# A decoder layer with experts: tokens sorted by kind for the middle layer, the row copies moved to ScalarE, and a memset between the result gathers

## The reference

```python
x = x + attn(_layernorm(x), wq, wk, wv, wo ...)      # 16 heads of 128, weights = codes * block scales
x = x + xattn(_layernorm(x), token_ids, ctx, ctx, ctx)
x = x + ffn(_layernorm(x), router_w, bias, w_gate, w_up, w_down, sw_gate, sw_up, sw_down)

# xattn: a feed-forward with 4 experts; the token's id picks one (the same ctx[e] serves as Wg, Wu, Wd)
expert_ids = min(clip(token_ids, 0, 12499) // 3125, 3)
for e in range(4):
    y = (silu(h @ ctx[e].T) * (h @ ctx[e].T)) @ ctx[e].T     # 256 -> 256 -> 256
    out = where(expert_ids == e, y, out)

# ffn: 32 experts 256 -> 128 -> 256, the best 4 of each token by sigmoid(h @ router_w.T) + bias,
# weighted by their scores over the scores' sum, plus one shared expert for all tokens
```

## Time and profile before

| | |
|---|---|
| median of 3 runs | 532.93 us (532.72 to 533.77) |
| the profiled execution | 531.99 us, its span 530.3 us |
| busy, share of the span | PE 94%, DVE 80%, ACT 55%, POOL 38% |
| bytes moved by DMA | 57.01 MB |

### The profile page before, as it was taken

How to read it: one execution, slowest core, us unless ns; L and a number is a source line. 1 busy time by engine, 2 the same in 40 slices (tenths; PEclk the granted TensorE clock), 3 DMA queues, 4 the chain that set the end, 5 groups by cost and what they waited for, 6 DMA issues and landing times.

```text
span 530.3 us, 11470 instructions
## 1 busy us (share of the span) xinstructions
PE 499.6 (94%) x3274; PEld 443.8 (84%) x3274; DVE 422.2 (80%) x1046; ACT 289.3 (55%) x793; POOL 201.5 (38%) x233
## 2 busy tenths in 40 slices
PE   7799999999999999999999998899987799999997
PEld 6688899899899899898898897678975588888886
DVE  6589988988988988988988987874688586677555
ACT  2566656656656655656666556254444244455552
POOL 3318621611612513513503600064510466627662
PEclk9999999999999999999999999999999999999999
DMA  6361311210210211211200792199921155436665
GB/s 192 99 170 40 92 32 32 69 30 30 69 30 30 69 30 30 69 30 30 69 0 1 257 323 96 26 296 305 297 69 41 43 147 159 160 110 184 192 187 166
DMA packets 59411, 57.01 MB, mean 108 GB/s; under 512 B 4128, under 2 KB 57072, under 8 KB 59248
## 3 DMA queue, kind: packets, MB, share of 16 engines
q1 hardware_dynamic: 55936, 48.03, 30.2%
q0 software_dynamic: 3168, 8.42, 6.1%
q10 hardware_dynamic: 272, 0.13, 0.1%
HBM read 46.21 MB, written 18.74 MB: 122 GB/s over the span
## 4 chain that ended last, share of the span: by engine, by line
PE 67%; DVE 19%; ACT 6%; issue 5%; POOL 1%; DVEq 0%; ACTq 0%; POOLq 0%
PE bank L791 14%; PE bank L792 13%; PE bank L793 13%; PE bank L965 11%; PE bank L973 5%; DVE rmax L1394 3%; DVE qk_lo L1386 3%; DVE nmax L1398 3%; PE bank L871 3%; ACT qk_hi L1190 2%; ACT prob L1198 2%; DVE pT_lo L1426 2%; PE bank L1146 1%; PE bank L969 1%; PE bank L797 1%
## 5 line engine op out<-in xcount | busy, mean ns | idle before, releaser
L1198 ACT ACTIVATE prob<-bank,nmax 128x256 f32<-128x256 f32 x128 | 59.5, 470 | 107.7 <-DVE nmax L1398 107.7
L607 POOL TENSOR_TENSOR w_lo<-st_c,w_hi 128x512 fp32r<-128x512 f32 x32 | 41.3, 1289 | 194.3 <-ACT w_hi L1161 194.3
L965 PE MATMUL bank<-moe_w,xT 128*128 x252 | 65.2, 381 | 1.2 <-DVE xT L1622 1.2
L1386 DVE SCALAR_TENSOR_TENSOR qk_lo<-bank,b_col,qk_hi 128x512 fp32r<-128x512 f32 x64 | 47.9, 748 | 16.0 <-ACT qk_hi L1190 15.3
L791 PE MATMUL bank<-hT_hi,w_lo 128*128 128x512 f32 x128 | 52.8, 413 | 5.8 <-DVE qk_lo L1386 2.9
L1394 DVE TENSOR_REDUCE rmax<-bank 128x2 f32<-128x512 f32 x64 | 43.9, 686 | 14.2 <-PE bank L793 14.1
L965 PEld LDWEIGHTS bank<-moe_w,xT 128*128 128x128 f32 x252 | 45.4, 190 | 6.8 <-issue 1.6
L689 POOL DMA_INDIRECT x_in<-h_dram,source x32 | 32.4, 1011 | 48.4 <-DVE source L1574 28.1
L792 PE MATMUL bank<-hT_lo,w_hi 128*128 128x512 f32 x128 | 50.7, 396 | 0.0
L793 PE MATMUL bank<-hT_hi,w_hi 128*128 128x512 f32 x128 | 50.4, 394 | 0.0
L1190 ACT ACTIVATE qk_hi<-bank,b_col 128x512 fp32r<-128x512 f32 x64 | 44.0, 687 | 7.7 <-PE bank L793 6.2
(11 more groups left out here) (219 smaller groups left out, 1543.3 us busy)
## 6 DMA issues: line engine op xcount, KB each, us to landing
y_dram<-ysb SPq DMA_DIRECT2D x63, 128.0 KB, 2.5
moe_w<-in_w_gate SPq DMA_DIRECT2D x8, 512.0 KB, 8.4
moe_w<-in_w_up SPq DMA_DIRECT2D x8, 512.0 KB, 7.6
moe_w<-in_w_down SPq DMA_DIRECT2D x4, 1024.0 KB, 8.8
st_c<-in_wq_codes SPq DMA_DIRECT2D x16, 128.0 KB
st_c<-in_wk_codes SPq DMA_DIRECT2D x16, 128.0 KB
st_c<-in_wv_codes SPq DMA_DIRECT2D x8, 256.0 KB
st_c<-in_wo_codes SPq DMA_DIRECT2D x8, 256.0 KB
```

The lines of the kernel that those rows point to most:

```text
L965: mm = pe.matmul(o, xT_of(kt), w, start=kt == 0, stop=kt == KT - 1)
L1198: ex = act.activation(prob[:, i % 4, qt, :], bS[i % 2][:, qt * S:(qt + 1) * S], ACT.Exp, bias=nmax[:, i % 2, qt:qt + 1], scale=SCALE, accu ...
L1386: dve.scalar_tensor_tensor(out=qk_lo[:, hp, m, n * HALF:(n + 1) * HALF], in0=src[:, :], scalar=b_col[:, bass.ds(g_h + m * H, 1)], in1=qk_h ...
```

## The change

**Sorting.** The token ids are loaded one for each partition and tile. GpSimd compares them (`kinds`), TensorE ranks them by matmuls with ones in the last attention group (`token_ranks`), GpSimd works out for each token its place in its half sorted by kind (`places`) and the borders of the kinds (`segments`). When a pair of residual tiles is complete, GpSimd scatters its rows with indirect DMAs to `xs_dram` in sorted order (`scatter`), and SP reads the tiles back into `x_acc`. VectorE then normalizes the first half after attention instead of between its last tiles; TensorE runs some matmuls whose result nobody uses meanwhile (`keep_warm`).

**The middle layer** has 14 segments (`NSEG`), 7 for each half: at each border of two kinds a tile is computed once for each. ScalarE copies the segment's tile (`segment_copy`, by a register), TensorE does 6 matmuls of 256 columns with the kind's weights, ScalarE silu, VectorE one operation with the segment's mask, TensorE two transposes (`mid`), ScalarE and VectorE split, TensorE 6 matmuls of 256 columns, VectorE adds to the residual (`routed_sum`). GpSimd only writes its constants. Normalization statistics are spread over the segments; half of the normalization for the third layer runs on GpSimd (`ln_pool`), and some square roots become powers on GpSimd (`ln_root`).

**The router** builds `in_slot` in four parts; the last shared-expert steps are placed behind the first row transpose and around the first expert product.

**The expert steps.** The row copies go to ScalarE. The store count lags one store instead of two (`AFTER`). Since the tokens are sorted now, the residual and the tables are written to `x2_dram` in trip 2 and gathered back by 8 indirect DMAs in the token's order, after which `order`, `slots_ordered`, `last_slots` and `tiles_needed` run, in trip 4 (`TABLE_TRIP`) instead of 1 and 2.

**The result gathers** wait for other product counts, and between two of them GpSimd clears one column and waits for that.

The diff, cut to its core:

```diff
+        BESIDE = 38
+            def own(ins):
+                done[0] += 1
+                ins.then_inc(p_own, 1)
+                pool.wait_ge(p_own, done[0])
...
+            def scatter(half):
+                pool.wait_ge(p_dest, 1)
+                for t in range(half * HT, (half + 1) * HT):
+                    if t % 2 == 0:
+                        pool.wait_ge(v_w, Plan(G - 1).w_done_count(t // 2, True))
+                    pool.indirect_dma_start(out=xs_dram, out_offset=bass.IndirectOffsetOnAxis(ap=dest[:, t:t + 1], axis=0),
+                                            in_=x_acc[:, t, :], in_offset=None).then_inc(d_xs[half], 16)
...
             for n in range(ROWS):
-                wait(pool, t_x, n - AHEAD + 1)
+                wait(pool, t_x, n - min(STEPS, 4 + n // 6) + 1)
                 pool.indirect_dma_start(out=xg[:, n % STEPS, :], ...
+            pool.wait_ge(d_x2, 16)
+            for t in range(NT):
+                pool.wait_ge(t_gu, SH + 3 * STEPS + t * 7 // 8)
+                pool.indirect_dma_start(out=x_all[:, t, :], out_offset=None, in_=x2_dram, ...
             pool.wait_ge(v_slot, S_NEED)
             for n, (t, k) in enumerate(gather_order):
+                if n > 0:
+                    own(pool.memset(quiet[:, :], 0.0))
                 if k == 2:
                     pool.wait_ge(t_x, ROWS)
                 if k == 3:
                     pool.wait_ge(v_sh, NT)
-                wait(pool, t_gu, SH + BESIDE + n)
+                pool.wait_ge(t_gu, SH + min(USED, BESIDE + n * 7 // 8))
                 if t % 2 == 0:
                     apart(pool)
                     pool.reg_load(at[0:2], need[0:1, k * NT + t:k * NT + t + 2])
...
# SP
+            for half in range(NH):
+                sp.wait_ge(d_xs[half], 16 * HT)
+                for t in range(half * HT, (half + 1) * HT):
+                    sp.dma_start(x_acc[:, t, :], xs_dram.rearrange("(t p) d -> t p d", p=P)[t]).then_inc(d_xa[t], 16)
             sp.wait_ge(v_w, 4 * G + 1)
+            sp.wait_ge(p_seg, 1)
...
# TensorE, middle layer
             def pre(n):
+                pe.wait_ge(a_copy, n + 1)
+                wait(pe, v_t, n - 1)
                 for kt in range(KT):
+                    mm = mm3(Z_AT[n % 2][:, 0:D], h_seg[:, n % 2, kt * P:kt * P + P], h_seg[:, n % 2, (KT + kt) * P:(KT + kt) * P + P],
+                             kind_part(cT_hi, n, kt), kind_part(cT_lo, n, kt), kt == 0, kt == KT - 1)
+            for n in range(NSEG + 2):
+                if n < NSEG:
+                    pre(n)
+                if n == NSEG:
+                    ln_tensor(pe, 2, 0, ENDS[0])
+                if 1 <= n <= NSEG:
+                    mid(n - 1)
+                if n >= 2:
+                    post(n - 2)
+                if n == SEGS - 2:
+                    ln_tensor(pe, 1, 1, ENDS[1])
...
# VectorE, middle layer
+            for n in range(NSEG):
+                routed_product(n)
+                if n >= 1:
+                    routed_low(n - 1)
+                if n >= 2:
+                    routed_sum(n - 2)
+                beside(n)
...
# VectorE, trips
+            trip(TABLE_TRIP, 0, False, {2: (table_back, lambda: order(0), lambda: order(2)),
+                                        3: (lambda: order(4), lambda: order(6), slots_ordered),
+                                        5: (last_slots,), 7: (tiles_needed,)})
...
# ScalarE, trips
+            def row_copy(j):
+                wait(act, t_x, j + 1)
+                act.copy(xT_all[:, :, j * SLOTS:(j + 1) * SLOTS],
+                         bX[j % 2][:, 0:D].rearrange("p (k s) -> p k s", k=KT)).then_inc(a_row, 1)
```

More of the change, by code:

```diff
@@ L50 @@
 ROW_TRIPS = ROWS // STEPS
-LAST_TRIP = 2
+TABLE_TRIP = 4
 HOT = NT // 2
@@ L572, in store @@
                         stored(u - AFTER + STEPS, it - 1)
-            store(0)
-            with sp.Fori(1, TRIPS - 1) as it:
+            for it in range(ROW_TRIPS):
+                store(it)
+            with sp.Fori(ROW_TRIPS, TRIPS - 1) as it:
                 store(it)
@@ L911, in _, with load_kinds @@
             over_groups(pe, body)
-            def zero(half):
-                for yb in ENDS[half]:
-                    pe.matmul(yb[:, :], zeros[:, :], zeros[:, 0:1].to_broadcast([1, HALF]), start=True, stop=True)
+            at = [pe.alloc_register(f"at{i}") for i in range(STEPS)]
+            def load_kinds(w):
+                apart(pe)
+                pe.reg_load(at[w % 2 * PACK:w % 2 * PACK + PACK],
+                            seg_expert[0:1, :, :].rearrange("p h i -> p (h i)")[:, w * PACK:(w + 1) * PACK])
@@ L1322, in _, with trip @@
                     shared_silu(n + 3)
+                if n >= SH - 3 and n < SH - 1:
+                    row_copy(n - SH + 3)
                 shared_copy(n)
-            def trip(it, first, last):
+            def trip(it, first, last, rows=0):
                 steps = LAST if last else STEPS
@@ L1328, in trip @@
                     j = it * STEPS + u
+                    if u < rows and j > 0:
+                        row_copy(j + 1)
                     if u < steps:
@@ L1406, in body @@
             def body(pl):
-                for i in range(PAIRS + (DRAIN + 2 if pl.last else 0)):
+                for i in range(PAIRS + (DRAIN + 1 if pl.last else 0)):
                     if i < PAIRS and not (pl.first and i == 0):
@@ L1446, in body @@
-                    if pl.last and i == PAIRS + 3:
-                        ln_low(dve, 1, 0, ENDS[0])
-            over_groups(dve, body)
-            statistics, variances, reciprocals, rows = ln_vector(dve, 1, 1, x_acc)
-            dve.wait_ge(v_w, 4 * G + 1)
+                    if pl.last and i == 2:
+                        dve.wait_ge(t_rank, 1)
+                        dve.tensor_copy(ranked[:, :], bO[0][:, S:S + NROUTE * NT + NROUTE * NH]).then_inc(v_rank, 1)
+                    if pl.last and i == 4:
+                        dve.wait_ge(p_bounds, 1)
+                        for half in range(NH):
+                            ins = dve.max(sorted_b[:, half, :], bounds[:, half, :])
+                        ins.then_inc(v_sorted, 1)
@@ new lines, in routed_low, with routed_sum @@
+            def routed_low(n):
+                dve.wait_ge(a_g, n + 1)
+                wait(dve, t_y, n - 1)
+                dve.tensor_tensor(gu_lo[:, n % 2, :], TURN_AT[n % 2][:, 0:D], gu_hi[:, n % 2, :], ALU.subtract).then_inc(v_g, 1)
+            def routed_sum(n):
+                row = dve.snap(at[word(n) % STEPS], min_val=0, max_val=(NT - 1) * (D + 2 * TOPK))
+                dve.wait_ge(t_y, n + 1)
+                wait(dve, v_y, n)
+                here = x_all[:, :, :].rearrange("p t d -> p (t d)")[:, bass.ds(row, D)]
+                apart(dve)
+                dve.tensor_tensor(here, y_at(n), here, ALU.add).then_inc(v_y, 1)
@@ L1452, in _ @@
+            norm = {(n, half): ln_vector(dve, n, half, x_acc) for n, half in LN_KINDS[2:]}
+            statistics, variances, reciprocals, rows = norm[1, 0]
             statistics()
             variances()
+            for tile in Plan(G - 1).of_slot(PAIRS + DRAIN, 1):
+                proj_low(Plan(G - 1), *tile)
             reciprocals()
@@ L1480, in _ @@
[L1480 to L1485 removed]
+                if n >= 2:
+                    routed_sum(n - 2)
+                beside(n)
+            routed_low(NSEG - 1)
+            routed_sum(NSEG - 2)
+            sums_ready(1, HT - 2)
+            routed_sum(NSEG - 1)
+            sums_ready(1, HT - 1)
@@ L1486, in _ @@
+            for part in norm[2, 1][1:]:
                 part()
@@ L1688, in add_shared, with trip @@
                 dve.tensor_tensor(x_acc[:, t, :], shared[:, t, :], x_acc[:, t, :], ALU.add).then_inc(v_sh, 1)
-            def trip(it, rows, last, beside, between={}):
+            def trip(it, rows, last, beside):
                 steps = LAST if last else STEPS
```

589 lines of the change are left out of this document (397 added, 192 removed).

## The result

The changed kernel takes **548.75 us** (median of four runs, 548.14 to 549.16) beside 533.35 us for the kernel before: a ratio of **1.0275, 95% interval 1.0232 to 1.0319**, slower. The profiled execution has a span of 546.9 us against 530.3.

What follows compares the result with a forecast made beforehand. TensorE, busy 94% of the span, was taken as the bound. Terms 4.0 - 19.9 - 4.8 = -20.7 us, plus 34.7 for the result gathers, on 531.99 profiled gave 546.0; median forecast 546.9 us, range 513 to 553.

Steps and rivals of the forecast that it cites:

- Part 1: End of attention: scatter, read-back, normalization and transposes ahead of the first middle matmul cost +4.0 us, bounds +1 and +6.
- Part 2: Middle layer: 14 segments take 30 us instead of 49.9, a gain of 19.9; bounds 26.5 and 36 us.
- Part 3: Router: spread statistics, slot masks in four parts and moved shared-expert steps gain 4.8 us of 31.3; bounds -2.5 and -6.
- Part 4: Expert steps: row copies, reordering gathers, table store and VectorE's table work all lie beside TensorE, so no change.
- Part 5: Result gathers on GpSimd: waiting for the memset exposes each gather's lead, pitch 2.3 us instead of 1.25, TensorE +34.7 us.
- TensorE's wait, 34.4 us: Last products: TensorE asks for the last gather at 526.4, it lands at 560.8; 0.3 us more for the restart.
- Rival 1: Result gathers: the lead stays hidden, pitch 1.25 to 1.55 us, time 514 to 523 us; chance 0.23.
- Rival 2: Middle layer: segments of 2.6 us make it 39 us, 556 in all; chance 0.07 together with Rival 3, over 553.
- Rival 3: Scatter and read-back waits drop TensorE's clock to 1.2 GHz for half the middle: 559 us; chance 0.07 together with Rival 2.

Runs made afterwards that it cites:

- the sequencer's own wait: Changed kernel with the memset left out but semaphore and wait kept, GpSimd's sequencer adding to the semaphore itself: 0.9977 of the kernel before (0.9954 to 1.0001).

## Why the prediction was right, and where not

The forecast was 546.9 us and the range 513 to 553, with slower at 0.68. The time is 548.75, 1.9 us above the forecast and 4.2 inside the range, and the mechanism is the one named. By its own steps:

- **Part 1, +4.0 us.** Measured +3.7: first middle matmul at 345.11, 345.4 forecast. The landings, booked at 2.9 us each, took 2.4 and 2.2 in the median, and the first transpose came at 340.80 instead of 341.6; from there to the first matmul it took 4.3 us instead of 3.8.
- **Part 2, 30 us.** Measured, to the start of the last add as in the 49.9 before, 375.29 - 345.11 = 30.2. Undisturbed segments, from 360 us on, are 1.64 us apart, where I had 1.75 to 1.8, and the early ones beside VectorE's normalization 1.95 to 2.85, where I had 2.1.
- **Part 3, 26.5 us.** Measured 402.15 - 375.29 = 26.9. The power on GpSimd, which I booked at nothing (+-0.3), takes 1.03 us, and from `var` to the use of its result it is 377.81 - 376.49 = 1.32. The root and reciprocal of the kernel before take 394.99 - 394.34 = 0.65 for the same:
```profile
394.34 0.17 DVE L728 TENSOR_SCALAR var<-mv 128x4 f32<-128x4 f32 x1
...
394.99 0.16 DVE L736 TENSOR_TENSOR nt<-rstd 128x4 f32<-128x4 f32 x1
```
  So that term was mis-sized by 0.7 us. This is read from rows; no run swapped the two. The net shift at the first expert product is 20.4 us, against 20.7.
- **Part 4, nothing.** This step failed, by 1.5 us. From the first to the last expert product it is 95.7 us against 94.2 before. VectorE's table work, which I booked as lying beside TensorE, comes in pieces of 1 us between the copies that the next product waits for; steps beside it are 1.9 us apart instead of 1.63 (418.71, 420.62, 422.50). That it fits beside TensorE is true of the mean and not of each step: the pieces are as long as VectorE's free time in a step, or longer. This is read from the timeline alone; the four slowest steps (416.79 to 424.58) make up 1.3 of the 1.5 us.
- **Part 5, pitch 2.3 us, bounds 1.9 and 2.5.** Measured 2.262, with an odd lead of 0.85 (I took 1.1) and an even one of 1.46 (1.44). The mean came nearer than its parts, because some even tiles take up to 1.9. The first gather was forecast at 486.5 - 20.7 = 465.8 and came at 468.40, 2.6 us late: the steps ahead lost up to 1.5 us, the shift ahead of them was 20.4 and not 20.7, and it starts 1.9 us after the table and not 1.4. The last was forecast at 537.1 and came at 538.53; TensorE starts on it at 541.38, 2.85 later, 3.0 forecast.
- **TensorE's wait, 34.4 us, and what stands behind it.** The waits for gathers sum to 30.6 us, but their sum is the wrong thing to compare: TensorE does part of its products between them, some at the lower clock, and neither moves the end. What sets the end is the last gather and the work behind it. Forecast: it lands at 560.8 - 20.7 = 540.1, and 4.2 us follow (530.3 - 526.4, and 0.3 for the restart), so 544.3. Measured: 541.38 and 5.5 us, 546.9. The products behind the last gather take 544.31 - 541.38 = 2.93 us; in the kernel without the memset, at a clock of 1.0, they take 512.91 - 511.36 = 1.55. So **1.4 us** is the lower clock, a term that I had put at nothing. (In the changed kernel's second trace, on the other chip, it is 544.21 - 541.90 = 2.31, so 0.8 us: there the eight products before still ran at 1.00.) My error: I had thought of the clock as a rival of the middle layer only, and not of the 30 us wait that my own forecast contained.

The span is 2.6 us above the forecast, 1.3 ahead of the last landing and 1.3 behind it. The 1.3 ahead are a first gather that comes 2.6 us late, less 31 x (2.3 - 2.262) = 1.2 for the pitch and 0.15 for the landing. The median misses by only 1.9, because I had added 0.9 for its distance from the profiled execution and it was 0.2. So part of the closeness is luck: in the pitch a lead 0.25 us too long for odd tiles met even tiles that sometimes take longer, and the clock's 1.4 us met smaller misses the other way.

Rival 1, at 514 to 523, needed the lead to stay hidden behind the wait for the own memset. The kernel without memset gives 518.0 us, so its price was right; its condition, a lead that stays hidden, doesn't hold. The rule that spoke for it, in the Trainium skill, "Perfetto Trace Analysis", on the SWDGE DMA instruction, says that the sequencer hands an instruction over and goes on to the next. The back-to-back gathers and the sequencer's own wait (0.30 us of gap) agree with it; the 0.85 us behind every late wait shows that the rule can't be stretched over a wait that isn't fulfilled yet. Rival 2 had no part: the middle took 30.2 us. Rival 3 didn't happen where it was looked for, because the change fills those waits with matmuls; with them taken out the clock fell there, and the middle took about 1 us longer.

## What to carry to other kernels

A wait cost nothing here where it was already fulfilled (gap 0.30 us), and little between small operations (0.08 us); ahead of an indirect DMA, and ending at the last moment, it cost 0.85 us and more. So before putting a wait between two DMAs of one engine, look for rows in which that engine was released by a semaphore, and count the gap after the release once per wait, not the length of the small operation. A constant gap whose releaser changes from row to row is such a lead. And when the sum of a forecast has a long wait on TensorE in it, the work behind the last such wait belongs in the sum at the lower clock (1.4 us here); slow work between waits only takes from the next wait.

## What the runs showed of the hardware that I had not expected

- Behind a wait that ends late, GpSimd's indirect DMA starts 0.85 us after the work waited for has ended, in every kernel that has the pair, for memsets of 0.11 and 0.33 us alike, and 1.46 with a register load in between. Behind a wait already fulfilled it starts 0.30 us after the gather ahead, and a memset of 0.12 us fits into that gap for nothing.
- After 25.5 us without work, eight products took 3.65 us instead of 1.99; 4 us later the clock was back, and four took 1.03. Waits of 2.30 and 1.95 us with eight products between brought it down again: the last four took 2.07. In another kernel idle stretches of 4.3 and 2.4 us brought it to 0.84 and 0.88 over the windows around them.
- The same wait for GpSimd's own operation costs 0.08 us ahead of a small operation of 128x4 elements.
- A power of 128x4 elements takes GpSimd 1.01 to 1.05 us, where a multiply of that size takes it 0.20 and a normalized tile of 128x256 1.22.
- On two of the four chips of the experiments ScalarE and GpSimd stand still in the expert steps for 1 to 5.4 us at a time, in seven of eight traces, with no releaser on record. DMAs move data during most of the longest one (133 GB/s). In three kernels the longest ends at nearly the same time, 491.2 to 491.7 us. The kernel before took 12 to 13 us longer on these chips. The cause stays open.
